# The second pass's last recurrent step worked by halves of its columns, in all eight groups

## The reference

```python
h = relu(adj @ (x @ Wg0 + bg0))
h = relu(adj @ (h @ Wg1 + bg1))
for p in 1..4:                       # the four passes
    nw = T // p
    wins = h[:, :nw*p].reshape(B*nw, p, H)
    last = lstm_last(Wih[p-1], Whh[p-1], ..., wins)   # p steps from a zero state
    h[:, idx] = last                 # idx = arange(nw)*p + p-1
# one step: i, f, gg, o = split(x_t @ Wih.T + h @ Whh.T + bias)
#   c = sigmoid(f)*c + sigmoid(i)*tanh(gg);   h = sigmoid(o)*tanh(c)
```

## Time and profile before

| what | us |
|---|---|
| median of 3 runs | 651.85 |
| lowest and highest | 651.63, 652.19 |
| the profiled execution's own time | 652.54 |
| its span in the profile | 650.7 |

### The profile page before, as it was taken

The page is one execution under the profiler, slowest core; times in us unless marked ns, Lnnn a source line. Parts: engine busy times, 40 slices in busy tenths (PEclk is TensorE's granted clock), DMA queues, the critical chain, the costliest instruction groups (busy, mean ns, idle before and its releaser), DMA issues.

```text
span 650.7 us, 9400 instructions
## 1 busy us (share of the span) xinstructions
PE 629.9 (97%) x2740; PEld 440.1 (68%) x2740; DVE 473.5 (73%) x1595; ACT 427.6 (66%) x953; POOL 174.3 (27%) x231
## 2 busy tenths in 40 slices
PE   9999999999999999999999999999999999999993
PEld 6756656447975686588668757955875786576573
DVE  4999999876947658876976787687778766464464
ACT  3567767957847765685776578567766856456562
POOL 2665551005332004114403230440313033021031
PEclk9999999999999999999999999999999999999998
DMA  8234000000000000000000000000000000000000
GB/s 339 112 129 163 1 2 2 0 0 2 2 2 0 1 1 1 1 2 33 1 1 33 1 1 2 34 0 2 1 33 1 2 34 0 2 0 34 0 34 33
DMA packets 4371, 16.83 MB, mean 26 GB/s; under 512 B 480, under 2 KB 480, under 8 KB 4192
## 3 DMA queue, kind: packets, MB, share of 16 engines
q1 hardware_dynamic: 4320, 16.23, 6.5%
HBM read 12.03 MB, written 4.19 MB: 25 GB/s over the span
## 4 chain that ended last, share of the span: by engine, by line
PE 71%; DVE 7%; ACT 4%; issue 2%; POOL 0%; ACTq 0%; DVEq 0%; POOLq 0%
PE QQ L786 26%; PE QQ L798 15%; PE PA L769 4%; PE PA L741 4%; PE PB L760 2%; PE PB L622 2%; PE PA L622 2%; PE PB L722 2%; PE PA L722 2%; ACT raw L1075 1%; PE PB L808 1%; DVE HB L1428 1%; PE PA L578 1%; PE PB L701 1%; PE PA L701 1%
## 5 line engine op out<-in xcount | busy, mean ns | idle before, releaser
L1075 ACT ACTIVATE raw<-QQ,BL 128x256 f32<-128x256 f32 (+4 forms) x312 | 167.8, 559 | 93.8 <-PE QQ L798 49.7
L786 PE MATMUL QQ<-HT,WT 128*128 128x256 f32 (+2 forms) x624 | 204.2, 472 | 3.5 <-DVE HT L1549 2.7
L413 POOL TENSOR_TENSOR RSD<-VAR,pw 128x8 f32<-128x8 f32 (+1 forms) x42 | 61.6, 1466 | 386.8 <-DVE VAR L1261 386.8
L786 PEld LDWEIGHTS QQ<-HT,WT 128*128 128x128 f32 x624 | 115.4, 190 | 69.2 <-issue 31.2
L798 PE MATMUL QQ<-HB,WT 128*128 128x256 f32 (+2 forms) x384 | 114.5, 441 | 1.8 <-DVE HB L1549 1.4
L798 PEld LDWEIGHTS QQ<-HB,WT 128*128 128x128 f32 x384 | 70.1, 190 | 35.9 <-issue 15.3
L1087 ACT ACTIVATE raw<-raw 128x256 f32<-128x256 f32 (+4 forms) x88 | 41.4, 471 | 30.0 <-DVE raw L1531 23.3
L1521 DVE SCALAR_TENSOR_TENSOR raw<-raw 128x512 f32<-128x512 f32 (+2 forms) x66 | 36.6, 555 | 24.0 <-ACT raw L1075 23.3
L1549 DVE SCALAR_TENSOR_TENSOR HB<-raw 128x256 f32<-128x256 f32 (+4 forms) x48 | 22.1, 461 | 23.9 <-ACT raw L1087 23.9
L919 ACT ACTIVATE X<-Z,OFF,RSD 128x128 f32<-128x128 f32 x80 | 31.8, 482 | 2.0 <-POOL OFF L419 2.0
L578 PE MATMUL PA<-AHT,X 128*128 128x256 f32 x128 | 29.5, 384 | 2.6 <-ACT X L919 2.4
(11 more groups left out here) (215 smaller groups left out, 1087.4 us busy)
## 6 DMA issues: line engine op xcount, KB each, us to landing
four<-in_x SPq DMA_DIRECT2D x8, 512.0 KB, 4.1
raw<-in_xt SPq DMA_DIRECT2D x8, 512.0 KB, 6.7
out<-four SPq DMA_DIRECT2D x7, 512.0 KB, 2.6
WT<-in_lstm SPq DMA_DIRECT2D x1, 2048.0 KB, 8.1
later<-in_later SPq DMA_DIRECT2D x1, 725.5 KB, 10.7
AD<-in_adj SPq DMA_DIRECT2D x2, 256.0 KB, 5.0
out<-four SPq DMA_DIRECT2D x2, 256.0 KB, 2.1
early<-in_early SPq DMA_DIRECT2D x1, 275.0 KB, 4.7
```

The source lines that it names most:

```text
L413: pool.tensor_tensor(RSD[kk][:, ts], VAR[kk][:, ts], pw[:, ts], ALU.pow).then_inc(ln[k]["rstd"], some)
L786: mm = pe.matmul(steps_view(Q[q], k), WT[:, 0, (p - 1) * 4 + q, :], ht_view(par, k), start=True, stop=(s == 0))
L1075: act.activation(TG[q][:, at:n], Q[q][:, at:n], ACT.Tanh, scale=0.5 if q == G else 0.25, bias=BL[:, p - 1, q:q + 1]).then_inc(g_ok, 1)
```

## The change

Step 3 (k = 3) takes the halved form in groups 0 to 5 too. `HALF_STEP = 3` is tested beside `g >= HALVED` in ACT's gates, ACT's cell tanh, DVE's state and DVE's choice of the cell function. `halved` counts one signal for each of the groups 0 to 5 and goes on from six for the groups 6 and 7. No step but k = 3 changes, and PE, GpSimd (POOL) and the DMA queues keep their instructions.

```diff
+HALF_STEP = 3
...
         def halved(g, k):
-            return NSTEP * (g - HALVED) + k + 1, FORGETS[NSTEP] * (g - HALVED) + FORGETS[k] + 1
+            if g < HALVED:
+                return g + 1, g + 1
+            return HALVED + NSTEP * (g - HALVED) + k + 1, HALVED + FORGETS[NSTEP] * (g - HALVED) + FORGETS[k] + 1
...
-                    if q == F and g >= HALVED:
+                    if q == F and (g >= HALVED or k == HALF_STEP):
                         at = middle(k)
                         act.activation(TG[q][:, 0:at], Q[q][:, 0:at], ACT.Tanh, scale=0.25,
                                        bias=BL[:, p - 1, q:q + 1]).then_inc(f_half, 1)
...
-                if g >= HALVED:
+                if g >= HALVED or k == HALF_STEP:
                     at = middle(k)
                     act.wait_ge(cell_half, halved(g, k)[0])
...
-                if g >= HALVED:
+                if g >= HALVED or k == HALF_STEP:
                     at = nw // 2
                     dve.wait_ge(tc_half, halved(g, k)[0])
...
-                        lstm_cell_halves(s - 2, k) if s - 2 >= HALVED else lstm_cell(s - 2, k)
+                        lstm_cell_halves(s - 2, k) if s - 2 >= HALVED or k == HALF_STEP else lstm_cell(s - 2, k)
```

## The result

| | before | changed |
|---|---|---|
| median, us | 651.74 (651.34 to 652.19, 4 runs) | 648.03 (647.64 to 648.19, 4 runs) |
| profiled execution's own time | 652.54 | 648.14 |
| its span | 650.7 | 646.4 |
| ratio, 95% interval | | 0.9942 [0.9929, 0.9954] |

The account below looks back on a forecast made before the run. PE, busy for 97% of the span, was taken as the bound, so time is won only where it waits. Six turns at 0.68 us make 4.1, taking the median from 651.85 to 647.8, range 646.8 to 649.3.

Parts of the forecast that it names:

- The stall and its chain: PE waits for DVE's step-3 state before `x(4)` and, by way of `a_max`, before `h(5)`: 0.79 us lost together.
- the first term: Step 3's chain from forget gate to state, halved as in group 6: 2.99 us instead of 3.67, 0.68 less.
- First wait gone, second wait left with 0.11: `x(4)` starts 0.47 us earlier without waiting; `h(5)` starts 0.68 earlier, at 275.06 where 274.95 was possible.
- The fourth rival: All of PE's loss before `h(5)` is won, restart included: 0.89 us a turn, 5.3 in all, 646.5; chance 0.05.
- After it, what `h(5)` gains, the turn gains: The only later state wait, 0.2 us before `x(2)`, moves along with PE's `x(1)`, so each turn gains 0.68.
- 0.32 more at the second: PE's loss at the wait before `h(5)`, beyond 0.47 us at the first wait, before `x(4)`: 0.79 together.
- One sign: Before `h(5)` in each of six turns, a weight load would wait some 0.1 to 0.2 us instead of 0.6.
- The first (step 4 follows PE): Rival: `h(5)` hangs on step 4's gates and gains only 0.47 us a turn: 2.8 in all, 649.0; chance 0.05.
- The second (something further down gives it back): Rival: a transfer or POOL result on its own clock later in the turn cancels the 0.68 us: 651.9; chance 0.04.
- The third (no overlap): Rival: each stage ends both halves before the next begins, chain 0.56 us longer, 3.4 in all: 655.2; chance 0.02.
- the rule weighed there: Fixed latency per DVE or ACT instruction speaks against 256-element pieces: 0.55 us a turn, 3.3 for six, if nothing overlapped.

Follow-up runs that it names:

- the repeat: The changed kernel run once more, beside the version with a_max's last two reductions moved, on the same chip: 648.32 us, ratio 0.9947 to the kernel before.
- head: Only the forget gate and CF halved in groups 0 to 5, CELL, tanh and state whole: 651.57 us, ratio 0.9992 to the kernel before.
- its waits in the better order: Only CELL, tanh and state halved, with DVE waiting for the forget gate first and the old cell second ahead of CF: 649.26 us, ratio 0.9965.
- tail only: Only CELL, tanh and state halved in groups 0 to 5, forget gate and CF whole: 650.28 us, ratio 0.9972 to the kernel before.

## Why the prediction was right

**The stall and its chain: right.** The wait of PE for step 3's state and the one before `h(5)` hung on one chain. The second did so by way of `a_max`: moving two reductions took it away and left the first as it was.

**The size of the first term: right.** 0.68 was taken from group 6 and the trace gave 3.67 - 2.99 = 0.68, by PE 0.69. It was right because group 6 runs the same shapes behind the same matmuls.

**First wait gone, second wait left with 0.11: right.** PE's start of `h(5)` came 4.10 after `x(4)`, 0.10 over the unhindered 4.00. The fourth rival was right that this rest can be won, but not by this change. It priced all of PE's loss at 0.89 a turn, and with the reductions moved as well a turn is 57.21 against 58.10 before (leaving the 0.08 aside): 0.89.

**"After it, what h(5) gains, the turn gains": right, with a term missing.** I said that the wait before `x(2)` moves along with its chain. It vanished instead in groups 1, 3 and 5. Each was worth 0.08. It is in the profiles only by the order in which DVE and POOL met in those executions. That 6 x 0.69 + 3 x 0.08 comes to 4.4 us, as far as the two profiled executions are apart, is luck. Matmul by matmul, the two traces also differ by 0.23 us in the first 7 us of the span and by 0.28 in the turn into group 6, and the last steps of groups 6 and 7 took 0.45 longer in the changed kernel; these three nearly cancel.

**One term has the wrong name.** The prediction puts 0.47 at the first wait and "0.32 more at the second". These 0.32 contain the 0.10 of the restart of `x(4)`: in the kernel before with the reductions moved, where `h(5)` doesn't wait, it still starts 274.56 - 270.46 = 4.10 after `x(4)`. So the second wait was 0.22, and the change won 0.47 at the first wait, 0.10 by the restart that went with it, and 0.11 at the second. The sum is the same.

**One sign was read wrongly.** I expected the weight load before `h(5)` to wait 0.1 to 0.2 us; it waited 0.48 where it had waited 0.58. Where nothing holds it, the load runs ahead of its matmul. Weight loads of `h(5)` in group 1, in the changed kernel and in that with the reductions moved:

```profile
274.08 1.44 PEld L803 LDWEIGHTS QQ<-HB,WT 128*128 128x128 f32 x6 [0.48 <-DVE HB L1554]
```

```profile
273.95 1.05 PEld L803 LDWEIGHTS QQ<-HB,WT 128*128 128x128 f32 x4
```

The second load starts 0.28 before its matmul (274.23) and has idled for 0.10 before that. These 0.38 are no loss to PE. Taken off, the waits of 0.58 and 0.48 are delays of 0.20 and 0.10, close to the 0.22 and 0.10 read from the matmuls' starts.

**The rivals.** The first (step 4 follows PE) fell with the changed kernel's own trace, where `h(5)` gained 0.69 and not 0.47, and with the moved reductions. The second (something further down gives it back) fell with the turns: all five are 0.68 to 0.69 shorter, apart from the 0.08. The third (no overlap) was built, and cost what it said: a chain longer by 0.51, forecast 0.56. That is also what became of the rule weighed there, from the Trainium skill, "VectorE: DVE Perf Modes", "The TRN2 errata": the estimate from its table was 0.55 a turn if nothing overlapped, and the trace agrees on the whole. Part by part it agrees for DVE (0.07 a pair against 0.06) and less for ACT, where the gate's pair costs 0.15 and the tanh's 0.42 + 0.33 - 0.63 = 0.12, against an estimate of 0.19 for each. The prediction took the row for SBUF for both; the gate reads PSUM. What the rule leaves out is the overlap. The Trainium skill has the other side too: "Perfetto Trace Analysis", "Optimizing Scalar/DVE Operations", says that where these engines aren't saturated but cause bubbles on others, breaking up instructions may let work finish sooner. The trace agrees: DVE is busy for 73% and ACT for 66%, and the chain got 0.68 us shorter.

**What stays open.** The profiled executions differ by 4.4 us, the medians by 3.7 and, in the repeat, 3.55. The intervals hold 4.1 each time. The profiled execution of the kernel before (652.54) was slower than each of its four other runs (at most 652.19), and 3 x 0.08 + 0.28 = 0.5 us of the 4.4 is the order in which DVE and POOL met. How often the unprofiled runs have either order isn't known, nor what makes the last steps of groups 6 and 7 differ by 0.45.

## What to carry over

A chain that passes between two engines stage by stage gets shorter by halving when each first half is signalled at once; the same halves without these signals made it longer by half a microsecond. Halve the whole chain or expect little: head and tail alone gave 0.08 and 0.34 of 0.68, the tail 0.42 with its waits in the better order. When the chain is as short as it gets, look at what stands between two waits in the queue: moving two reductions behind the next step's cell gave another 1.2 us by the traces and 1.45 by the medians on one chip.

## What the hardware showed that was not expected

- The order of two waits ahead of a DVE instruction matters. In tail only, with the late one last, CF starts 0.10 us after ACT's end; with an already met one behind it, 0.03 after.
- DVE's operations on two SBUF operands and POOL's scalings hold each other up: DVE takes 0.42 or 0.58 us for the same instruction, and POOL 2.47 or 2.16 for four scalings, which take 1.74 where DVE has no such operation beside them. In 72 places of twelve traces the one that pays changes from POOL to DVE where POOL's record starts 0.016 to 0.019 us ahead of DVE's. The Trainium skill, "SBUF — State Buffer", "SBUF: two separate sides", calls the shared ports an exclusive lock that goes to whichever starts first. The traces agree as to the order: with POOL later by 0.11 us DVE never paid, and with POOL ahead by 0.019 us or more it always did.
- PE pays 0.10 us to restart after the waits before `x(4)` and `h(5)`: 4.27 against 4.17 for 14 matmuls, 2.55 against 2.45 for eight.
